# Deformable 3x3 convolution on one core: sampling in five matmuls instead of six, two row groups completed by small DMAs, and a new order of the steady iteration

## The chip, the cores and the metric

The kernel runs on one core of a Trainium2 chip. The metric is the device time of one execution in microseconds. Matrix products run on TensorE (PE, with its weight loads PEld), elementwise work on VectorE (DVE), ScalarE (ACT) and GpSimd (POOL), and DMAs are issued from the queues of SyncE (SP) and ScalarE (ACTq).

## The reference

Two layers on x of 64 images, 1024 channels, 14x14 pixels, all float32. Layer 0 is a residual bottleneck (1x1, 3x3, 1x1 convolutions with batch norms); it is done before the part that changes. Layer 1, cut to what matters:

```python
out = relu(group_norm(conv(x, w1)))                      # 1024 -> 256 channels
om = conv(out, w_off, pad=1) + b_off                     # 27 channels: 9 x offsets, 9 y offsets, 9 masks
py, px = grid_y + ky + off_y, grid_x + kx + off_x        # for each of K = 9 taps and 196 pixels
sampled = bilinear_sample(out, py, px) * sigmoid(mask)   # [256, 9, 14, 14] per image
out = einsum('bckhw,ock->bohw', sampled, w2)             # 9 taps x 256 channels -> 256
out = conv(relu(group_norm(out)), w3)                    # 256 -> 1024
return relu(group_norm(out) + x)
```

## The kernel before

Layer 1 is `deformable_phase`. It works on pairs of images (32 pairs), software-pipelined: `by_iteration` runs one `step` per pair, and each engine's `step` is a hand-written list of calls for the pairs `past`, `before`, `now`, `after`, `coming`. The order inside each engine is exactly that list; engines meet only through semaphores. (The pairs are named alike on every engine but shifted: what PE calls `now` and `after` in its last lines is `before` and `now` for ACT and DVE.)

Every product is made in three passes of float32r parts: a value is split by ACT into a high part and by DVE into the rest, and high x high, low x high and high x low are added in PSUM.

Bilinear sampling is a matrix product. For a pair, an image i and a group g of two taps (the fifth group has one), the matrix s of 196 source pixels x (2 taps x 196 target pixels) is the product of a "hat" in y and a "hat" in x. A unit u is one (g, i): nine units a pair, and the last holds the single tap of both images. A unit goes through these steps:

- `load_hats` (SP): the hats are read from DRAM (`hat_scratch`) and spread over the partitions, into one of three buffers `hats`. With the 196 pixels in two halves of 98 partitions (7 image rows of 14) that is three DMAs: y hats of each half, x hats.
- `make_s` (POOL for units 0, 1, 2, 6, 7, DVE for 3, 4, 5, 8) multiplies y hats by x hats.
- `part_s` (ACT) makes s_hi, `rest_s` (DVE) s_lo; the next load into the same buffer waits for s_lo.
- `sample_tile` t (PE), 20 a pair: t = 4g + 2i + c, c being the half of the 256 channels. The weights are aT, the image's activations transposed (`transposes`, `part_aT`, `rest_aT`), the moving operand is s. Six matmuls: two halves of the pixels by three products, each over 98 partitions. Tiles 0 to 15 have 392 columns, 16 to 19 have 196.
- `part_v` (ACT) and `rest_v` (DVE) take each tile out of PSUM; `deform_part` (PE) multiplies by w2.

A pair's hats begin when `spread_offsets` has spread the offsets: ACT makes distances, hats and mask, POOL multiplies the mask in (`mask_hats`), SP stores them to `hat_scratch` (`store_hats`), waits for that, and loads units 0, 1, 2. Around this, PE also does conv1 (`conv1` 0 to 7) of a later pair, the offset convolution (`offsets`), and the last 1x1 convolution (`conv3` 0 to 7) of an earlier one, with one small matmul for each group norm (`group_a`, `group_b`, `group_y`).

## Time and profile before

| | |
|---|---|
| median of 3 runs | 2962.01 us (2961.58 to 2963.43) |
| the profiled execution | 2961.04 us, span 2958.8 us |
| mean granted clock of TensorE | 0.994 |
| busy share PE, PEld, DVE, ACT, POOL | 98%, 97%, 80%, 61%, 15% |
| mean share of the 16 DMA engines | q1 (SP) 32.7%, q10 (ACTq) 11.8% |

The span runs from the first to the last instruction; the execution's own time is 2.2 us longer. The deformable stage fills the last two thirds, from about 960 us on, and is a steady iteration repeated for each pair.

### The profile page before, as it was taken

The numbers are of one execution on the slowest core, as the hardware profiler recorded it, in microseconds if no ns is written. First come the engines' busy times: TensorE is split into PE (matmuls) and PEld (weight loads), VectorE is DVE, ScalarE is ACT, GpSimd is POOL, SyncE is SP. The second block draws the span as 40 slices with busy tenths as digits, with TensorE's granted clock in tenths as the row PEclk, the third lists the DMA queues.
The fourth block names the chain that finished last, engine by engine and source line by source line (L and its number), as shares of the span: only waits on it lengthen the run. The fifth ranks groups of instructions, "written<-read, shape, count | busy, mean of one in ns | idle before, by whom it ended". The sixth has DMA issues, their size and how long they took to land.

```text
span 2958.8 us, 46593 instructions
## 1 busy us (share of the span) xinstructions
PE 2908.3 (98%) x16518; PEld 2865.9 (97%) x16518; DVE 2366.0 (80%) x5000; ACT 1795.0 (61%) x3281; POOL 455.3 (15%) x305
## 2 busy tenths in 40 slices
PE   9999999999998999999999999999999999999997
PEld 9999999999997899999999999999999999999997
DVE  5655889865666688888888888888888888888885
ACT  4544332346665466767666676676766767667664
POOL 0000000000000122221222212222122221222210
PEclk9999999999999899999999999999999999999998
DMA  7774111035663344444444444444544444444431
GB/s 270 215 238 134 44 44 40 10 124 218 245 232 130 122 136 152 156 150 158 150 153 154 148 159 151 153 155 150 158 150 156 152 149 159 148 152 156 149 121 74
DMA packets 209208, 437.39 MB, mean 148 GB/s; under 512 B 18640, under 2 KB 170192, under 8 KB 203344
## 3 DMA queue, kind: packets, MB, share of 16 engines
q1 hardware_dynamic: 159408, 326.82, 32.7%
q10 hardware_dynamic: 49568, 107.60, 11.8%
q8 instruction: 131, 2.15, 0.3%
q14 instruction: 101, 0.83, 0.1%
HBM read 307.71 MB, written 126.64 MB: 147 GB/s over the span
## 4 chain that ended last, share of the span: by engine, by line
PE 63%; DVE 3%; DMA 1%; ACT 1%; SPq 0%; issue 0%; POOL 0%; ACTq 0%; DVEq 0%; POOLq 0%
PE sample L87 7%; PE deform L87 7%; PE sample L88 7%; PE sample L92 7%; PE deform L92 7%; PE deform L88 6%; PE work L87 6%; PE work L92 6%; PE work L88 6%; PE work L74 1%; PE work L76 1%; PE work L75 1%; DMA hats<-hat_scratch 1%; PE work L2046 1%; DVE x L1715 1%; DVE s_lo L1819 1%
## 5 line engine op out<-in xcount | busy, mean ns | idle before, releaser
L1465 ACT ACTIVATE v_hi<-sample 128x392 fp32r<-128x392 f32 (+1 forms) x640 | 291.7, 463 | 315.1 <-PE sample L92 306.0
L87 PE MATMUL sample<-s_hi,aT_hi 98*128 98x392 f32 (+1 forms) x1280 | 417.5, 331 | 8.9 <-DVE v_lo L1827 8.9
L1675 POOL TENSOR_TENSOR hats<-hats 98x784 f32<-98x784 f32 x160 | 341.0, 2131 | 523.1 <-DMA hats<-hat_scratch 504.3
L88 PE MATMUL sample<-s_hi,aT_lo 98*128 98x392 f32 (+1 forms) x1280 | 413.3, 328 | 0.0
L87 PE MATMUL deform<-v_hi,w_w 128*128 128x392 f32 x1152 | 403.5, 350 | 0.0
L88 PE MATMUL deform<-v_hi,w_w 128*128 128x392 f32 x1152 | 393.1, 341 | 0.0
L1827 DVE TENSOR_TENSOR v_lo<-sample,v_hi 128x392 fp32r<-128x392 f32 (+1 forms) x640 | 326.9, 518 | 66.5 <-ACT v_hi L1465 62.2
L92 PE MATMUL sample<-s_lo,aT_hi 98*128 98x392 f32 (+1 forms) x1280 | 315.1, 327 | 0.0
L92 PE MATMUL deform<-v_lo,w_w 128*128 128x392 f32 x1152 | 310.4, 342 | 0.0
L1456 ACT ACTIVATE s_hi<-hats 98x784 fp32r<-98x784 f32 x288 | 245.4, 852 | 98.5 <-DVE x L1715 71.7
L1819 DVE TENSOR_TENSOR s_lo<-hats,s_hi 98x784 fp32r<-98x784 f32 x288 | 281.1, 976 | 2.4 <-ACT s_hi L1456 1.4
L87 PEld LDWEIGHTS sample<-s_hi,aT_hi 98*128 98x128 f32 x1280 | 241.6, 189 | 13.6 <-DVE v_lo L1827 6.1
L88 PEld LDWEIGHTS sample<-s_hi,aT_lo 98*128 98x128 f32 x1280 | 243.0, 190 | 0.1
L92 PEld LDWEIGHTS sample<-s_lo,aT_hi 98*128 98x128 f32 x1280 | 227.3, 189 | 0.3 <-DVE s_lo L1819 0.3
L88 PEld LDWEIGHTS deform<-v_hi,w_w 128*128 128x128 f32 x1152 | 217.8, 189 | 0.0
L87 PEld LDWEIGHTS deform<-v_hi,w_w 128*128 128x128 f32 x1152 | 217.6, 189 | 0.0
L1715 DVE SCALAR_TENSOR_TENSOR x<-in_home,scale,x 128x392 f32<-128x392 f32 x248 | 210.2, 848 | 5.5 <-DMA in_home<-y_scratch 5.5
L92 PEld LDWEIGHTS deform<-v_lo,w_w 128*128 128x128 f32 x1152 | 211.8, 188 | 0.0
L1843 DVE SCALAR_TENSOR_TENSOR x<-y_home,gn,x 128x196 f32<-128x196 f32 x496 | 208.5, 483 | 0.1
L1141 POOL TENSOR_TENSOR gn<-gn,half_neg 128x2 f32<-128x2 f32 x96 | 76.4, 796 | 810.0 <-DVE gn L1153 810.0
L1521 ACT ACTIVATE x<-x,gn 128x196 f32<-128x196 f32 x496 | 191.6, 447 | 1.0 <-issue 0.6
L1388 ACT ACTIVATE x<-x,shift 128x392 f32<-128x392 f32 x256 | 157.8, 616 | 46.4 <-DVE x L1715 33.2
(227 smaller groups left out, 7282.9 us busy)
## 6 DMA issues: line engine op xcount, KB each, us to landing
hats<-hat_scratch SPq DMA_DIRECT2D x768, 150.1 KB
x<-in_x SPq DMA_DIRECT2D x64, 784.0 KB, 5.8
in_home<-y_scratch ACTq DMA_DIRECT2D x248, 196.0 KB, 3.3
out<-x ACTq DMA_DIRECT2D x62, 784.0 KB, 4.4
y_home<-in_x SPq DMA_DIRECT2D x32, 784.0 KB, 5.0
y_scratch<-y_out SPq DMA_DIRECT2D x16, 1568.0 KB, 5.9
terms<-in_x SPq DMA_DIRECT2D x30, 784.0 KB, 4.7
y_scratch<-y_home SPq DMA_DIRECT2D x15, 1568.0 KB, 5.1
```

The lines of the kernel that those rows point to most:

```text
L87: nc.tensor.matmul(out, w_hi, x_hi, start=start, stop=False)
L88: nc.tensor.matmul(out, w_lo, x_hi, start=False, stop=False)
L92: return nc.tensor.matmul(out, w_hi, x_lo, start=False, stop=stop)
L1388: nc.scalar.activation(x1[:, p.buf, :, k, :], x1[:, p.buf, :, k, :], ACT.Relu, bias=shift[:, k:k + 1]).then_inc(x1_made, 1)
L1456: nc.scalar.activation(s_hi[:, unit % 2], hats[:, unit % HATS, 0:2], ACT.Copy).then_inc(s_hi_made, 1)
L1465: nc.scalar.activation(v_hi[:, group % 2, c, 0:taps_of(g), i, :], sample[:, t % 2, 0:cols(g)].rearrange("p (k s) -> p k s", s=PIX), ACT.Co ...
L1521: last = nc.scalar.activation(x1[:, p.buf, i, k, :], x1[:, p.buf, i, k, :], ACT.Relu, bias=gn3.shift[:, i, k:k + 1])
L1675: nc.gpsimd.tensor_tensor(hats[:, slot, 0:2, 0:n], hats[:, slot, 0:2, 0:n], hats[:, slot, 2:3, 0:n].broadcast_to([HALF, 2, n]), ALU.mult). ...
L1715: nc.vector.scalar_tensor_tensor(x1[:, p.buf, :, k, :], from_y, scale[:, k:k + 1], x1[:, p.buf, :, k, :], ALU.mult, ALU.add).then_inc(plus ...
L1819: nc.vector.tensor_tensor(s_lo[:, unit % 2], hats[:, unit % HATS, 0:2], s_hi[:, unit % 2].bitcast(F32), ALU.subtract).then_inc(s_lo_made, 1)
L1827: nc.vector.tensor_tensor(v_lo[:, group % 2, c, 0:taps_of(g), i, :], sample[:, t % 2, 0:cols(g)].rearrange("p (k s) -> p k s", s=PIX), v_h ...
L1843: last = nc.vector.scalar_tensor_tensor(x1[:, p.buf, i, k, :], y[:, i, k, :], gn3.scale[:, i, k:k + 1], x1[:, p.buf, i, k, :], ALU.mult, A ...
```

## The change

The 196 source pixels are no longer cut 98 + 98 but 126 + 70: 9 image rows and 5. The first group (A) keeps its three products. Of the second (R, 70 rows) the three products are packed into two matmuls. Plane 2 of the weights has the high part of aT on rows 0 to 69, and on rows 70 to 125 the low part of rows 0 to 55; its moving operand has s_hi of R on rows 0 to 69 and again s_hi of R's rows 0 to 55 on 70 to 125 (the y hats of those rows are loaded a second time, so `make_s`, `part_s` and `rest_s` make the copy with the same instructions, on 126 partitions instead of 98). Plane 3 has the high part on rows 0 to 69 with s_lo, and on rows 70 to 83 the low part of rows 56 to 69 with s_hi. What must cross partitions for this is moved by DMA from SBUF to SBUF: `copy_s`, 14 rows of 392 per unit, and `copy_aT`, 56 and 14 rows per image. The moved rows of s have semaphores of their own, taken over from the earlier phases (`first_loaded0` and `3`), those of aT use `last_counted`. Each hats load is four DMAs (9, 5 and 4 rows of y hats, x hats over 9 rows). `rest_aT` becomes two instructions, and the low part of R goes to `a_f`'s place first. The order of the steady iteration is another one on PE, ACT, DVE and SP (POOL's is the same); the first and the last iterations follow it.

```diff
-        aT_hi = sb("aT_hi", [HALF, 2, 2, CMID], F32R)
-        aT_lo = sb("aT_lo", [HALF, 2, 2, CMID], F32R)
+        aT = sb("aT", [A_ROWS, 2, 4, CMID], F32R)
...
-        hats = sb("hats", [HALF, HATS, 3, 2 * PIX])
-        s_hi = sb("s_hi", [HALF, 2, 2, 2 * PIX], F32R)
-        s_lo = sb("s_lo", [HALF, 2, 2, 2 * PIX], F32R)
+        hats = sb("hats", [A_ROWS, HATS, 3, 2 * PIX])
+        s_hi = sb("s_hi", [A_ROWS, 2, 2, 2 * PIX], F32R)
+        s_lo = sb("s_lo", [A_ROWS, 2, 2, 2 * PIX], F32R)
...
+                for i, at in parts:
+                    n = at.stop - at.start
+                    y_hat, x_hat = (hats_at[p.n % 2, e, i, :, t0:t0 + n] for e in range(2))
+                    for dst, rows in ((hats[:, slot, 0, at], slice(0, UPPER)), (hats[0:R_ROWS, slot, 1, at], slice(UPPER, SIDE)),
+                                      (hats[R_ROWS:A_ROWS, slot, 1, at], slice(UPPER, SIDE - 1))):
+                        sp.dma_start(dst, y_hat[rows].unsqueeze(1).broadcast_to([rows.stop - rows.start, SIDE, n])
                                      ).then_inc(hats_loaded[slot], 16)
...
+                    sp.dma_start(hats[:, slot, 2, at], x_hat.unsqueeze(0).broadcast_to([UPPER, SIDE, n])
                                  ).then_inc(hats_loaded[slot], 16)
...
+            @of_pair
+            def copy_s(p, u):
+
+                unit = UNITS * p.n + u
+                sp.wait_ge(s_lo_made, unit + 1)
+                sp.dma_start(s_lo[R_ROWS:C_ROWS, unit % 2, 1].bitcast(F32), s_hi[TWICE:R_ROWS, unit % 2, 1].bitcast(F32)
+                             ).then_inc(s_moved[unit % 2], 16)
+
+            @of_pair
+            def copy_aT(p, i):
+
+                sp.wait_ge(aT_lo_made, 2 * p.n + i + 1)
+                if i == 1:
+                    sp.wait_ge(aT_moved, aT_moved_before + 64 * p.n + 32)
+                for plane, rows in ((2, slice(0, TWICE)), (3, slice(TWICE, R_ROWS))):
+                    n = rows.stop - rows.start
+                    sp.dma_start(aT[R_ROWS:R_ROWS + n, i, plane].rearrange("p (k c) -> p k c", k=KM).bitcast(F32),
+                                 aT_rest[rows, :, i].bitcast(F32)
+                                 ).then_inc(aT_moved, 16)
...
-                for h in range(2):
-                    products_of_high(nc, sample[:, t % 2, 0:n], aT_hi[:, i, h, c * P:(c + 1) * P],
-                                     aT_lo[:, i, h, c * P:(c + 1) * P], s_hi[:, unit % 2, h, at:at + n], start=(h == 0))
+                to, a_part = sample[:, t % 2, 0:n], aT[:, i, :, c * P:(c + 1) * P]
+                high, low = s_hi[:, unit % 2, :, at:at + n], s_lo[:, unit % 2, :, at:at + n]
+                nc.tensor.matmul(to, a_part[:, 0], high[:, 0], start=True, stop=False)
+                nc.tensor.matmul(to, a_part[:, 1], high[:, 0], start=False, stop=False)
+                if t in (0, 2):
+                    pe.wait_ge(aT_moved, aT_moved_before + 64 * p.n + 32 * (i + 1))
+                nc.tensor.matmul(to, a_part[:, 2], high[:, 1], start=False, stop=False)
                 if c == 0:
                     pe.wait_ge(s_lo_made, unit + 1)
-                for h in range(2):
-                    last = product_of_low(nc, sample[:, t % 2, 0:n], aT_hi[:, i, h, c * P:(c + 1) * P],
-                                          s_lo[:, unit % 2, h, at:at + n], stop=(h == 1))
+                nc.tensor.matmul(to, a_part[:, 0], low[:, 0], start=False, stop=False)
+                if c == 0:
+                    pe.wait_ge(s_moved[unit % 2], s_moved_before[unit % 2] + 16 * (unit // 2 + 1))
+                last = nc.tensor.matmul(to, a_part[0:C_ROWS, 3], low[0:C_ROWS, 1], start=False, stop=True)
```

SP's list of the steady iteration, where every `copy_` line is new and `load_x` moved:

```diff
             def step(past, before, now, after, coming):
+                copy_s(now, 1)
                 load_hats(now, 4)
+                copy_s(now, 2)
                 load_hats(now, 5)
+                copy_s(now, 3)
+                load_x(coming, 0)
+                copy_s(now, 4)
                 load_hats(now, 6)
                 load_hats(now, 7)
-                load_x(coming, 0)
+                copy_s(now, 5)
+                load_x(coming, 1)
                 load_hats(now, 8)
-                load_x(coming, 1)
                 store_hats(after, 1, 0)
+                copy_s(now, 6)
                 store_hats(after, 1, 1)
+                copy_s(now, 7)
                 store_hats(after, 0, 0)
                 store_hats(after, 0, 1)
                 load_hats(after, 0)
+                copy_s(now, 8)
                 load_hats(after, 1)
                 load_hats(after, 2)
+                copy_aT(after, 0)
+                copy_s(after, 0)
                 load_hats(after, 3)
+                copy_aT(after, 1)
```

One 392-column sample tile on PE, the first of a unit, before (in brackets what it waits for):

```order
L87 MATMUL sample<-s_hi,aT_hi 128x392 [waits v_lo_made,s_hi_made]
L88 MATMUL sample<-s_hi,aT_lo 128x392
L87 MATMUL sample<-s_hi,aT_hi 128x392
L88 MATMUL sample<-s_hi,aT_lo 128x392
L92 MATMUL sample<-s_lo,aT_hi 128x392 [waits s_lo_made]
L92 MATMUL sample<-s_lo,aT_hi 128x392
```

The same on PE after the change, tile 0 of a pair, where the wait for the moved rows of aT (`last_counted`) and of s (`first_loaded0`) stands too:

```order
L2107 MATMUL sample<-s_hi,aT 128x392 [waits v_lo_made,s_hi_made,aT_lo_made]
L2108 MATMUL sample<-s_hi,aT 128x392
L2111 MATMUL sample<-s_hi,aT 128x392 [waits last_counted]
L2114 MATMUL sample<-s_lo,aT 128x392 [waits s_lo_made]
L2117 MATMUL sample<-s_lo,aT 128x392 [waits first_loaded0]
```

One matmul is gone, and the tile has two waits that end only with a DMA.

SP's queue from the last hats store of a pair to the load of unit 3, before:

```order
L1339 DMA hat_scratch<-offs_b 9x14x196 [waits masked] x2
L1327 DMA hats<-hat_scratch 98x1x392 [waits hats_stored0,s_lo_made]
L1327 DMA hats<-hat_scratch 98x1x392
L1330 DMA hats<-hat_scratch 98x1x392
L1327 DMA hats<-hat_scratch 98x1x392 [waits hats_stored1,s_lo_made]
L1327 DMA hats<-hat_scratch 98x1x392
L1330 DMA hats<-hat_scratch 98x1x392
L1327 DMA hats<-hat_scratch 98x1x392 [waits s_lo_made]
L1327 DMA hats<-hat_scratch 98x1x392
L1330 DMA hats<-hat_scratch 98x1x392
```

The same place on SP after the change, from the load of unit 1 to the first copy of s, with the copy of unit 8 of the pair before ahead of it:

```order
L1345 DMA s_lo<-s_hi 14x392 [waits s_lo_made]
L1335 DMA hats<-hat_scratch 126x1x392 [waits hats_stored1,s_lo_made]
L1335 DMA hats<-hat_scratch 70x1x392
L1335 DMA hats<-hat_scratch 56x1x392
L1337 DMA hats<-hat_scratch 126x1x392
L1335 DMA hats<-hat_scratch 126x1x392 [waits s_lo_made]
L1335 DMA hats<-hat_scratch 70x1x392
L1335 DMA hats<-hat_scratch 56x1x392
L1337 DMA hats<-hat_scratch 126x1x392
L1356 DMA aT<-in_home 56x2x128 [waits aT_lo_made]
L1356 DMA aT<-in_home 14x2x128
L1345 DMA s_lo<-s_hi 14x392 [waits s_lo_made]
```

Four DMAs stand where three stood, and the three small moves for sample tile 0 stand behind the twelve of units 0, 1 and 2.

## Rows read from the trace of the kernel before

**Rows 1.** Page, part 1: busy time of the engines over the whole span.
```profile
span 2958.8 us, 46593 instructions
PE 2908.3 (98%) x16518; PEld 2865.9 (97%) x16518; DVE 2366.0 (80%) x5000; ACT 1795.0 (61%) x3281; POOL 455.3 (15%) x305
```

**Rows 2.** Windows: length, busy us PE, PEld, DVE, ACT, POOL, PEclk, DMA share, GB/s.
```profile
2000.00:2250.00 250.00, 250.00 (x1466) 248.79 (x1465) 217.90 (x512) 174.25 (x356) 58.26 (x38) 1.00 0.48 153
```

**Rows 3.** Waits, 2000 to 2250 us: us in total, times, longest.
```profile
POOL hats L1675 <- DMA hats<-hat_scratch: 68.0, 18, 7.7
DVE v_lo L1827 <- ACT v_hi L1465: 5.3, 10, 1.4
```

**Rows 4.** Timeline of PE: start, us, engine, line, operation.
```profile
2000.06 0.34 PE L88 MATMUL deform<-v_hi,w_w 128*128 128x392 f32 x1
2000.24 0.34 PE L87 MATMUL deform<-v_hi,w_w 128*128 128x392 f32 x1
...
2000.96 0.25 PE L87 MATMUL sample<-s_hi,aT_hi 98*128 98x196 f32 x1
...
2001.61 0.27 PE L87 MATMUL sample<-s_hi,aT_hi 98*128 98x196 f32 x1
...
2007.93 0.34 PE L87 MATMUL sample<-s_hi,aT_hi 98*128 98x392 f32 x1
...
2009.01 0.34 PE L87 MATMUL sample<-s_hi,aT_hi 98*128 98x392 f32 x1
...
2049.42 0.34 PE L2035 MATMUL work<-x_hi,select_s 96*126 96x392 f32 x1
...
2062.53 0.26 PE L87 MATMUL sample<-s_hi,aT_hi 98*128 98x196 f32 x1
```

**Rows 5.** Groups by line and form, whole span.
```profile
L87 PE MATMUL sample<-s_hi,aT_hi 98*128 98x392 f32 x1024 | 355.6, 347 | 8.9 <-DVE v_lo L1827 8.9
```

**Rows 6.** Timeline of SPq: issues of stores, hats loads and an x load.
```profile
2037.32 0.45 SPq L1302 DMA_DIRECT2D x<-in_x  x1
...
2050.48 3.16 SPq L1339 DMA_DIRECT2D hat_scratch<-offs_b  x4
2054.77 1.55 SPq L1327 DMA_DIRECT2D hats<-hat_scratch  x2
2056.36 0.73 SPq L1330 DMA_DIRECT2D hats<-hat_scratch  x1
```

**Rows 7.** Timeline of POOL: `make_s` of units 0, 1, 2.
```profile
2060.75 1.88 POOL L1675 TENSOR_TENSOR hats<-hats 98x784 f32<-98x784 f32 x1 [7.37 <-DMA hats<-hat_scratch]
2064.52 1.89 POOL L1675 TENSOR_TENSOR hats<-hats 98x784 f32<-98x784 f32 x1 [1.89 <-DMA hats<-hat_scratch]
2067.36 2.59 POOL L1675 TENSOR_TENSOR hats<-hats 98x784 f32<-98x784 f32 x1 [0.94 <-DMA hats<-hat_scratch]
```

**Rows 8.** Timeline of DVE: L1715 alone and beside POOL, the split of aT.
```profile
2020.73 0.62 DVE L1715 SCALAR_TENSOR_TENSOR x<-in_home,scale,x 128x392 f32<-128x392 f32 x1
...
2061.16 1.90 DVE L1715 SCALAR_TENSOR_TENSOR x<-in_home,scale,x 128x392 f32<-128x392 f32 x1
...
2064.74 0.69 DVE L1801 TENSOR_TENSOR aT_lo<-work,aT_hi 98x512 fp32r<-98x512 f32 x1 [0.63 <-ACT aT_hi L1448]
2065.35 0.35 DVE L1827 TENSOR_TENSOR v_lo<-sample,v_hi 128x196 fp32r<-128x196 f32 x1
```

**Rows 9.** Windows of 2 us, columns as in rows 2.
```profile
2055.00:2057.00 2.00, 2.00 (x13) 2.00 (x12) 2.00 (x6) 1.97 (x5) 0.00 (x0) 1.00 0.45 135
2057.00:2059.00 2.00, 2.00 (x14) 1.95 (x14) 2.00 (x6) 1.97 (x6) 0.00 (x0) 1.00 0.45 140
...
2089.00:2091.00 2.00, 2.00 (x13) 2.00 (x13) 0.98 (x1) 0.99 (x2) 0.00 (x0) 1.00 0.94 329
```

**Rows 10.** DMA view, 2000 to 2250 us: packets, queues, issues (KB each, median us to landing).
```profile
DMA packets 22078, 38.28 MB, mean 153 GB/s; under 512 B 1778, under 2 KB 20008, under 8 KB 22056
...
in_home<-y_scratch ACTq DMA_DIRECT2D x33, 196.0 KB, 3.2
```

More of the change, by code:

```diff
@@ L1563, in second @@
                 part_a(after)
+                part_v(now, 6)
                 part_s(now, 5)
@@ L1864, in second @@
                 rest_s(now, 1)
-                make_s(now, 3)
+                rest_s(now, 2)
                 rest_v(now, 0)
@@ L1905, in step @@
                     return second(now, after, coming)
+                rest_x1(after, 1)
+                add_y(after, 3)
+                add_y(after, 4)
+                rest_s(now, 0)
                 rest_v(before, 16)
+                rest_v(before, 17)
                 rest_aT(now, 0)
-                rest_v(before, 17)
-                add_y(after, 3)
-                rest_x1(after, 1)
-                rest_s(now, 0)
+                add_x1(past, 5)
+                add_x1(past, 6)
                 rest_v(before, 18)
+                rest_aT(now, 1)
@@ L1913, in step @@
                 rest_v(before, 19)
-                add_x1(past, 5)
+                add_y(after, 5)
+                rest_s(now, 1)
+                add_x1(past, 7)
                 rest_x1(after, 2)
-                add_y(after, 4)
-                rest_aT(now, 1)
-                rest_s(now, 1)
+                rest_x1(after, 3)
+                add_y(after, 6)
+                rest_s(now, 2)
                 rest_v(now, 0)
                 rest_v(now, 1)
-                rest_x1(after, 3)
-                make_s(now, 3)
@@ L2133, in step @@
                     fresh = None
+                first = coming is not None and coming.n == 0
                 sample_tile(now, 16)
@@ L2155, in step @@
                 sample_tile(after, 5)
-                deform_part(after, 0, 1)
-                group_b(now)
-                if now is not None and now.n == PAIRS - 1:
-                    keep_warm(nc, sample[:, 0, 0:PAIR], w1.hi_flat, 26)
-                deform_part(after, 0, 2)
-                conv1(fresh, 4)
                 conv1(fresh, 5)
-                deform_part(after, 0, 3)
                 conv1(fresh, 6)
                 conv1(fresh, 7)
-                sample_tile(after, 6)
+                deform_part(after, 0, 1)
                 conv3(now, 0)
                 conv3(now, 1)
-                first = coming is not None and coming.n == 0
                 if first:
@@ L2175, in step @@
                 conv3(now, 2)
+                if now is not None and now.n == PAIRS - 1:
+                    keep_warm(nc, sample[:, 0, 0:PAIR], w1.hi_flat, 26)
+                deform_part(after, 0, 2)
                 conv3(now, 3)
+                conv3(now, 4)
+                sample_tile(after, 6)
                 sample_tile(after, 7)
-                conv3(now, 4)
-                sample_tile(after, 8)
-                deform_part(after, 1, 0)
                 conv3(now, 5)
```

279 lines of the change are left out of this document (141 added, 138 removed).

## The prediction

> **What bounds the kernel now.** I read the page's busy times first: PE has 98% of the span, DVE 80%, ACT 61% [rows 1]. An average over stages proves little, so next the windows of the deformable stage: over 250 us PE is busy for all 250 at full clock, DVE for 217.9 (87%), ACT for 174, and the DMA engines have a mean share of 0.48 [rows 2]. A busy PE can still hide waits, so the list of waits in that window: no row has PE as the one who waits; POOL waits for its hats, DVE 5.3 us for ACT [rows 3]. The timeline says the same: 392-column matmuls start 0.18 us apart, and tile 16 of one pair starts at 2000.96, that of the next at 2062.53 [rows 4]. So an iteration is **61.57 us**, all of it PE's matmul stream.
>
> **What goes.** A 392-column tile took 6 matmuls in 2009.01 - 2007.93 = 1.08 us, 0.18 each; a 196-column one 2001.61 - 2000.96 = 0.65 us, 0.108 each [rows 4]. One matmul of each goes. A pair has 16 wide tiles and 4 narrow ones: 1024 records of the wide form are 512 wide tiles with two halves each [rows 5], and 32 pairs have 128 narrow ones. 16 x 0.18 + 4 x 0.108 = 3.31 us per pair, **106 us** in all. A PE-bound iteration is then 61.57 - 3.31 = 58.26 us. That the five run over 126 rows of weights (the last over 84) instead of 98 I cost at nothing: deform's matmuls over 128 rows start 0.18 us apart too [rows 4]. If every one cost 5% more, 100 matmuls x 0.009 = 0.9 us a pair would come back.
>
> **What is added on DVE.** The same instructions on 126 partitions instead of 98 have the same columns; nothing. `rest_aT` becomes two instructions of 256 columns: 512 columns took 0.69, 196 took 0.35 [rows 8], so a line through both gives 0.41 each, 0.13 more per image, 0.26 per pair. DVE goes from 217.9 / 250 x 61.57 = 53.7 to 53.9 us of 58.26, or 93%. Its idle time falls from 7.9 to 4.3 us. Part of the busy time is collision: `add_y` (L1715) takes 0.62 alone and 1.90 when it starts 0.4 us after a POOL multiply, ending 0.4 us after that one's end [rows 7, 8]. The new order moves these calls about; one collision more or less is some 1.3 us, and with 4.3 us of idle time I take it as hidden.
>
> **What is added on SP.** A hats load issued three DMAs in 1.55 + 0.73 = 2.28 us; four stores took 3.16, an x load 0.45 [rows 6]. Now 8 units x 4 + 8 = 40 hats DMAs x 0.76 = 30.4, 3.2 for stores, 0.9 for x. The 9 copies of s and 4 of aT have no row: from 0.45 (plain x load) to 0.79 (one store), 6 to 10 us; I take 0.45 for s, plain like the x load, and 0.7 for aT, three-dimensional like hats: 6.9. Sum 41 us of 58: not a bound, but each unit is issued 0.76 us later.
>
> **What is added on the DMA engines.** With only hats moving, the share is 0.45 at 135 to 140 GB/s, against 0.94 at 329 GB/s when full rows move [rows 9]. 0.45 x 16 = 7.2: a hats DMA (7 image rows of 14 partitions) works on seven engines, and a backlog of further hats DMAs does not widen it to others. The small packets confirm it: 1778 under 512 B in 250 us are 438 per iteration [rows 10], and 30 hats DMAs x 7 + 4 stores (9 groups) x 9 + 12 others x 16 is exactly 438. At 137 GB/s one hats DMA (98 rows of 1568 B, 154 KB) takes 1.12 us. By the same pattern the new ones split in groups of 9, 5, 4 and 9 engines with 14 rows each, again 1.12 us. If the four meet on the same engines, a unit takes 4.5 us instead of 3.4. If they spread, about 3.4 remains; I take the first, since the seven never changed in the backlog.
>
> The Trainium skill has this as a rule (DMA: Bandwidth & Descriptors, section "Why a DMA increments its semaphore by 16 and not by 1"): a DMA from SP or ACT is split over the largest number up to 16 that divides the slowest dimension of both sides, and on the lowest-numbered engines. By it engines 0 to 3 carry all four DMAs, so it speaks against this change; the trace agrees on the number (7.2 of 16 by share), and cannot show which ones.
>
> Load of the fullest engine, per iteration: hats before 24 x 1.12 + 6 x 0.56 = 30.2 us. An x load or an output store of an image (803 KB) at 329 GB/s is 2.44 us on all 16, four of them 9.8; eight y loads of 201 KB, 4.9; stores 2.2. Sum 47.1 of 61.57 (76%). After: hats 32 x 1.12 + 8 x 0.56 = 40.3, copies about 1, sum **58.2 of 58.26**. Taken literally this is a second bound at the same height. It is an upper estimate: peaks of a busy stretch count gaps between DMAs as work, and 0.94 was not full. Spread evenly the new bytes would be far below. I do not let it set the time, but it is the place where the forecast can break.
>
> **The tight chain: from the offsets to tile 0.** Before: the last spread matmul at 2049.42; the first hats load is issued at 2054.77, 5.35 later; unit 2 is landed when POOL starts on it at 2067.36, 12.6 us after that [rows 4, 6, 7]. Tile 0 of the pair started 2007.93 - 2000.96 = 6.97 into its iteration, so at 2062.53 + 6.97 = 2069.50: 20.1 us after the spread. After: counting the matmuls of PE's new list at 0.18, the last spread is at 42.8 and tile 0 at 8.1 of the next iteration, 58.26 - 42.8 + 8.1 = 23.6 us. SP's first load now stands behind two copies of s (units 6 and 7), and hats are made after the mask: I count 1.9 us more, 7.2. Three units take 12.6 + 3 x 1.12 = 16.0. The copies of aT and of s for tile 0 are issued behind them and land no earlier, some 0.5 us later: 7.2 + 16.0 + 0.5 = 23.7. PE asks for them at its third and fifth matmul, 23.6 + 0.36 and + 0.72. That leaves 0.3 us for aT: no cover. The smallest landing in the trace is 3.2 us for 196 KB [rows 10], and 14 rows can hardly be slower; SP issues them when DVE has finished `rest_aT`, about 4 us ahead of need, so alone they fit. What is late next, if they are late, is tile 0, and with it everything behind on PE, 1 for 1. Similar short covers: the group_b matmul, which now stands 5.0 us (before 8.6) behind the last `deform_part` whose result must be copied, counted and reduced; and tile 18, which needs rest of tile 16 while `rest_s(0)` stands in front. I take **0.5 us of PE stall per iteration** for all, 31 x 0.5 = 15 us; bounds 0 and 3.3 (gain gone).
>
> **Sum.** 2961.0 of the profiled execution - 106 + 15 = 2870; that run is 1 us under the median, so **2871 us** on it, 3.1% faster.
>
> **The rivals.**
> A. The chain is later than I counted: DMAs of the hats or the small moves come 1 to 2.5 us late each iteration. For it: 58.2 of 58.26 on the fullest engine, and covers under 1 us. Against: POOL, DVE and ACT have room to take up jitter. At 1.5 us a pair, 2856 + 31 x 1.5 = 2903; span 2887 to 2935.
> B. DVE becomes the bound. If its forced idle time stays at 7.9 us although the order is new, the iteration is 53.9 + 7.9 = 61.8 and nothing is won; if it shrinks to 6, 59.9 us, 2856 + 51 = 2907. It decides above 4.3 us. Against: most of its idle time stood in waits for a PE that will be faster.
> C. Slower: the fullest DMA engines set the period. 36 wide-equivalents of hats DMA plus 17.9 us of the rest pass 61.57 at 1.21 us each, 8% above 1.12. At 1.25 the iteration is 62.9, 2962 + 32 x 1.3 = 3004. Against: 1.12 already has gaps in it, and it needs all four DMAs of a unit on the same engines. The Trainium skill's rule named above would put them there.
> D. The gain isn't there: five matmuls with 126 rows cost what six did. 2962. Against: deform's cadence with 128 rows.
>
> **How the numbers follow.** Forecast (stall 0 to 1 us a pair, 2856 to 2887) 0.65; A 0.20; B 0.08, of which 0.02 ends within 0.2%; C 0.05; D 0.02, half within 0.2%, half slower. Faster by over 0.2% (6 us, about what a measurement of this kernel tells from no change) 0.65 + 0.20 + 0.06 = 0.91; within it 0.02 + 0.01 = 0.03; slower 0.05 + 0.01 = 0.06. The range is 2852 to 2925: below, no stall and the 9 us that PE waited for v_lo over the whole span [rows 5] half gone; above, most of A and B.
>
> **What would show it.** Matmul records of tiles with five members 0.18 us apart; `transposes` or tile 16 repeating every 58.3 to 59.3 us; DVE about 92% busy in steady windows; DMA share about 0.6 and hats-only stretches above 0.45; POOL starting units 0, 1, 2 about 4.5 us apart. A stall shows as an idle row before the sample matmuls with a DMA as its releaser (chain, A), before group sums or sample with DVE (B). The forecast is wrong if the iteration is over 59.5 us, and most likely so if the copies of tile 0 land after the hats of unit 2 by more than 1 us.

## The result, and the profile after

The changed kernel takes **2986.39 us** (median of 4 runs, 2980.93 to 2989.8) against 2961.8 for the kernel before on the same chip: a ratio of 1.0081 (95% interval 1.0063 to 1.0098), so 0.8% slower. The profiled execution took 2985.33 us, of which 2983.1 are the span. The forecast was 2871, faster.

The page after, part 1, and the 250 us window of the deformable stage (columns as in [rows 2]):

```profile
span 2983.1 us, 46209 instructions
PE 2847.9 (95%) x15878; PEld 2753.8 (92%) x15878; DVE 2397.7 (80%) x5064; ACT 1807.6 (61%) x3345; POOL 463.3 (16%) x305
```

```profile
2000.00:2250.00 250.00, 240.43 (x1368) 232.09 (x1367) 220.90 (x521) 174.03 (x361) 56.35 (x36) 1.00 0.57 176
```

PE lost 60 us of work over the span, and the span grew by 24: what was all work in [rows 2] now has nearly 10 us of gaps in 250. (A matmul that starts after a wait is shown longer, 0.45 instead of 0.34 us in a row below, so busy PE fell by less than the work that went.) Who waits for what over the steady stage, 1250 to 2750 us: in total us, times, longest. First the engines, then SP's queue:

```profile
POOL hats L1716 <- DMA hats<-hat_scratch: 689.6, 121, 13.3
...
PE sample L2107 <- DVE v_lo L1871: 28.2, 42, 1.4
...
PE sample L2117 <- DMA s_lo<-s_hi: 20.4, 33, 1.8
...
PE sample L2111 <- DMA aT<-in_home: 10.3, 19, 1.0
```

```profile
SPq L1345 <- DVE s_lo L1863: 226.0, 87, 9.3
SPq L1356 <- DVE in_home L1845: 63.0, 24, 3.4
```

59 us of PE's gaps in 1500 have three releasers, none dominant: the rest of an earlier tile (`v_lo`; a tile may only be written once the tile two before it has been taken out), the moved rows of s, those of aT. For PE the same list of the kernel before holds 1.1 us for `v_lo` and nothing else. SP now waits at L1345 (`copy_s`, for `s_lo`) and L1356 (`copy_aT`, for the rest of R), with stores and loads of the next pair queued behind it. One iteration in detail. SP after, the columns of [rows 6]:

```profile
2058.54 0.80 SPq L1366 DMA_DIRECT2D hat_scratch<-offs_b  x1
2059.38 0.81 SPq L1345 DMA_DIRECT2D s_lo<-s_hi  x1
2060.23 0.76 SPq L1366 DMA_DIRECT2D hat_scratch<-offs_b  x1
2061.04 1.04 SPq L1345 DMA_DIRECT2D s_lo<-s_hi  x1
2062.12 1.57 SPq L1366 DMA_DIRECT2D hat_scratch<-offs_b  x2
2064.83 2.21 SPq L1335 DMA_DIRECT2D hats<-hat_scratch  x3
...
2067.88 0.83 SPq L1345 DMA_DIRECT2D s_lo<-s_hi  x1
...
2074.10 0.75 SPq L1337 DMA_DIRECT2D hats<-hat_scratch  x1
2077.91 1.76 SPq L1356 DMA_DIRECT2D aT<-in_home  x2
2079.72 0.81 SPq L1345 DMA_DIRECT2D s_lo<-s_hi  x1
```

POOL, DVE and PE in the same iteration (their timelines, one fence each):

```profile
2058.59 1.02 POOL L1723 TENSOR_TENSOR offs_b<-offs_b 126x392 f32<-126x392 f32 x1 [1.97 <-ACT offs_b L1475]
...
2072.54 2.20 POOL L1716 TENSOR_TENSOR hats<-hats 126x784 f32<-126x784 f32 x1 [11.27 <-DMA hats<-hat_scratch]
```

```profile
2072.39 2.78 DVE L1756 SCALAR_TENSOR_TENSOR x<-in_home,scale,x 128x392 f32<-128x392 f32 x2
2075.67 0.97 DVE L1863 TENSOR_TENSOR s_lo<-hats,s_hi 126x784 fp32r<-126x784 f32 x1 [0.50 <-ACT s_hi L1497]
...
2077.47 0.41 DVE L1845 TENSOR_TENSOR in_home<-work,aT 70x256 fp32r<-70x256 f32 x1
```

```profile
2077.06 0.33 PE L2107 MATMUL sample<-s_hi,aT 126*128 126x196 f32 x1 [0.83 <-DVE v_lo L1871]
...
2082.17 0.34 PE L2108 MATMUL sample<-s_hi,aT 126*128 126x392 f32 x1
2082.42 0.45 PE L2111 MATMUL sample<-s_hi,aT 126*128 126x392 f32 x1
```

Read as one chain: the mask product at 2058.59; four stores with two copies of s between them, done at 2063.69; first load at 2064.83; unit 0's product at 2072.54, and beside it two `add_y` that take 2.78 us instead of some 1.2; `s_lo` of unit 0 only at 2075.67, in front of the rest of tile 16 and the rest of R. So PE waits 0.83 us at 2077.06, where tile 18 needs the rest of tile 16, and SP stands from 2074.85 to 2077.91 until it may copy aT. Tile 0's third matmul is the first to read that copy; it starts at 2082.42, 0.25 us after the one at 2082.17 instead of 0.18, so here the copy came 0.07 us late. Tile 18 of the pair before waited likewise and started at 2014.18, so this iteration takes 62.9 us where 58.8 were forecast. This chain ends in only a part of its waits: between the two starts PE also waits 0.67 us for aT, 0.29 for `v_lo`, and 1.08 and 0.34 for copies of s.

### The profile page after: what moved, and what is told of

It reads as the page before. It is cut to its first block, busy times and chain, and to the rows that moved or that the text cites. A ratio compares the mean times of both kernels' runs of the same rounds, so it can differ in the third digit from the quotient of the medians.

```text
span 2983.1 us, 46209 instructions
## 1 busy us (share of the span) xinstructions
PE 2847.9 (95%) x15878; PEld 2753.8 (92%) x15878; DVE 2397.7 (80%) x5064; ACT 1807.6 (61%) x3345; POOL 463.3 (16%) x305
## 4 chain that ended last, share of the span: by engine, by line
PE 32%; DMA 14%; SPq 8%; DVE 8%; ACT 4%; issue 2%; POOL 2%; ACTq 0%; POOLq 0%; DVEq 0%
DMA s_lo<-s_hi 6%; PE work L92 4%; PE work L97 4%; PE work L93 4%; SPq L1335 3%; DMA hats<-hat_scratch 3%; PE deform L92 3%; PE deform L97 3%; PE deform L93 3%; DVE s_lo L1863 3%; PE sample L2117 2%; DMA aT<-in_home 2%; SPq L1356 2%; PE sample L2111 2%; PE sample L2107 2%
## 5 line engine op out<-in xcount | busy, mean ns | idle before, releaser
L1716 POOL TENSOR_TENSOR hats<-hats 126x784 f32<-126x784 f32 x160 | 328.8, 2055 | 922.1 <-DMA hats<-hat_scratch 922.1
L1863 DVE TENSOR_TENSOR s_lo<-hats,s_hi 126x784 fp32r<-126x784 f32 x288 | 311.8, 1083 | 34.4 <-ACT s_hi L1497 34.4
L1497 ACT ACTIVATE s_hi<-hats 126x784 fp32r<-126x784 f32 x288 | 245.9, 854 | 84.8 <-POOL hats L1716 79.8
L2107 PE MATMUL sample<-s_hi,aT 126*128 126x392 f32 (+1 forms) x640 | 216.3, 338 | 42.1 <-DVE v_lo L1871 41.9
L2117 PE MATMUL sample<-s_lo,aT 84*128 84x392 f32 (+1 forms) x640 | 218.4, 341 | 33.8 <-DMA s_lo<-s_hi 33.3
L2111 PE MATMUL sample<-s_hi,aT 126*128 126x392 f32 (+1 forms) x640 | 215.1, 336 | 14.4 <-DMA aT<-in_home 14.1
L97 PEld LDWEIGHTS deform<-v_lo,w_w 128*128 128x128 f32 x1152 | 211.8, 188 | 0.0
L2108 PE MATMUL sample<-s_hi,aT 126*128 126x392 f32 (+1 forms) x640 | 210.2, 328 | 0.0
L2114 PE MATMUL sample<-s_lo,aT 126*128 126x392 f32 (+1 forms) x640 | 210.2, 328 | 0.0
L1756 DVE SCALAR_TENSOR_TENSOR x<-in_home,scale,x 128x392 f32<-128x392 f32 x248 | 188.0, 768 | 13.9 <-DMA in_home<-y_scratch 13.5
L1146 POOL TENSOR_TENSOR gn<-gn,half_neg 128x2 f32<-128x2 f32 x96 | 97.0, 1010 | 601.5 <-DVE gn L1158 601.5
L92 PE MATMUL work<-b_hi,w3b_w 128*128 128x392 f32 x512 | 179.3, 350 | 4.9 <-ACT b_hi L1531 4.9
L2107 PEld LDWEIGHTS sample<-s_hi,aT 126*128 126x128 f32 x640 | 121.6, 190 | 62.7 <-issue 56.4
```

Source lines behind the costliest of these rows:

```text
L92: nc.tensor.matmul(out, w_hi, x_hi, start=start, stop=False)
L97: return nc.tensor.matmul(out, w_hi, x_lo, start=False, stop=stop)
L1497: nc.scalar.activation(s_hi[:, unit % 2], hats[:, unit % HATS, 0:2], ACT.Copy).then_inc(s_hi_made, 1)
L1716: nc.gpsimd.tensor_tensor(hats[:, slot, 0:2, 0:n], hats[:, slot, 0:2, 0:n], hats[:, slot, 2:3, 0:n].broadcast_to([A_ROWS, 2, n]), ALU.mult ...
L1863: nc.vector.tensor_tensor(s_lo[:, unit % 2], hats[:, unit % HATS, 0:2], s_hi[:, unit % 2].bitcast(F32), ALU.subtract).then_inc(s_lo_made, 1)
L2107: nc.tensor.matmul(to, a_part[:, 0], high[:, 0], start=True, stop=False)
```

## The experiments

Each kernel was timed against the kernel before on the same chip (2960 to 2961 us). "Period" is a median over 21 to 23 iterations, 1300 to 2700 us, from one mask product on POOL to the next; it is 61.56 us in the kernel before and 61.97 after (means 61.7 and 62.1). From the first to the last mask product the change costs 13 us of its 24; the other 11 lie behind the last one, where the pipeline runs out.

**1. Which part costs: the moves, the lists, or the five matmuls.** The edits are applied to the changed kernel.

```diff
 no_copy_s:  def copy_s(p, u):   + return      ; PE's wait on s_moved left out
 no_copy_aT: def copy_aT(p, i):  + return      ; PE's and ACT's waits on aT_moved left out
-    a_part[:, 2], high[:, 1]   ...  a_part[0:C_ROWS, 3], low[0:C_ROWS, 1]
+    a_part[0:R_ROWS, 2], high[0:R_ROWS, 1] ... a_part[0:R_ROWS, 3], low[0:R_ROWS, 1]
 no_copies:  both
```

> The changed kernel without both kinds of small move (the 9 copies of s and the 4 of aT per pair) and without PE's waits for them; the third and fifth matmul of a tile run over 70 rows, so part of the low products is left out. Theory 1 (the moves land late because they stand in SP's queue behind hats loads, and PE waits for them): most of the loss goes, 2860 to 2895 us. Theory 2 (the four hats DMAs of a unit share their engines, so the hats themselves are late): the hats still hold tile 0, 2930 to 2970. Theory 3 (the new order on DVE and ACT is the bound, the moves are innocent): 2970 to 2990.

> Only the copies of s and PE's wait for them are left out (the fifth matmul multiplies whatever low part stands on the 14 rows); those of aT stay. Theory 1: the copies of s are nine of the moves and the ones the last chain names most, so more than half of the difference goes, 2890 to 2930 us. Theory 2: 2950 to 2975. Theory 3: 2970 to 2990.

> Only the copies of aT and the waits for them are left out; the low products of the second group are left out with them, the third and fifth matmul run over 70 rows, and the nine copies of s stay as DMAs with PE's wait. Theory 1: tile 0 and tile 2 wait less, SP is free 3.5 us earlier before unit 3, 2940 to 2965 us. Theory 2: 2960 to 2980. Theory 3: 2970 to 2990.

Measured: without any move **2897.44** us (0.9793, 0.9776 to 0.9809), without those of s 2902.59 (0.9808, 0.9794 to 0.9823), without those of aT 2965.44 (1.0019, 1.0008 to 1.003). The moves cost 89 us; those of s alone 84, those of aT alone 21, so together less than the sum. The first is 2 us above theory 1's range, the last is just past theory 1's and inside theory 2's. (Without the moved rows a part of the low products of R is left out too; the number of matmuls stays five.) SP's issues without moves:

```profile
2068.24 3.13 SPq L1368 DMA_DIRECT2D hat_scratch<-offs_b  x4
2072.70 2.19 SPq L1335 DMA_DIRECT2D hats<-hat_scratch  x3
```

The mask product stood at 2068.30 there: 4.4 us to the first load, against 6.2 above. Over all iterations the medians are 4.50 without moves, 4.55 with those of aT alone, 5.99 after. The period is 59.25, 59.50 and 61.97.

The rest, 2897 against 2871, made the lists themselves suspect. So the new lists alone, with the six matmuls, buffers and three loads of before; and the reverse, packing and moves in the lists of before, each copy put in ahead of a load.

> The kernel before with the new order of the lists on PE, ACT, DVE and SP and nothing else: six matmuls, 98 + 98 partitions, three hats DMAs, no copies. Theory 1 (the order is innocent): PE has 3.3 us more work per pair and covers what it covered, 2960 to 2968 us. Theory 2 (the order itself brings waits of 1 us or more per pair): 2985 to 3010.

> The changed kernel (five matmuls, 126 partitions, four hats DMAs, all copies) with the lists of the kernel before, the copies put into SP's list each where its wait is met first. If the new order was needed to hide the moves (theory 1 with the order as a help): slower than the change, 3000 to 3050 us. If the new order was made for other latencies than the chip has and hurts (theory 2): faster than the change, 2930 to 2975.

Measured: the lists alone **3002.68** us (1.0142, 1.0127 to 1.0157), 41 us slower than before, as theory 2 had it. The packing in the old lists 3502.33 (1.1828, 1.1809 to 1.1848): slower than either theory, since PE waits for over half of the moves of s, up to 6.2 us each. The old lists have no room for them.

```profile
PE sample L2117 <- DMA s_lo<-s_hi: 251.5, 111, 6.2
```

Step by step that is 2961 + 41 (lists) - 105 (3003 to 2897: five matmuls, 126 partitions, the fourth load) + 89 (moves) = 2986. These are differences along one row of kernels, so they must add up; it is no proof that each term would have this size elsewhere, and part 2 shows that it doesn't.

**2. What in the lists costs.** POOL of the run with the lists alone, then DVE:

```profile
2021.92 1.95 POOL L1675 TENSOR_TENSOR hats<-hats 98x784 f32<-98x784 f32 x1 [1.03 <-DMA hats<-hat_scratch]
...
2060.31 1.88 POOL L1675 TENSOR_TENSOR hats<-hats 98x784 f32<-98x784 f32 x1 [1.51 <-DMA hats<-hat_scratch]
```

```profile
2022.06 2.78 DVE L1715 SCALAR_TENSOR_TENSOR x<-in_home,scale,x 128x392 f32<-128x392 f32 x2
2024.76 0.96 DVE L1819 TENSOR_TENSOR s_lo<-hats,s_hi 98x784 fp32r<-98x784 f32 x1
2025.65 0.62 DVE L1827 TENSOR_TENSOR v_lo<-sample,v_hi 128x196 fp32r<-128x196 f32 x2
...
2060.43 2.59 DVE L1819 TENSOR_TENSOR s_lo<-hats,s_hi 98x784 fp32r<-98x784 f32 x1
```

```profile
2026.14 0.33 PE L87 MATMUL sample<-s_hi,aT_hi 98*128 98x196 f32 x1 [0.62 <-DVE v_lo L1827]
```

In these rows a VectorE operation with both operands in SBUF that starts inside a product of GpSimd ends only after it: `s_lo` from 60.43 to 63.02, where the product ended at 62.19 and `s_lo` alone takes 0.97. The Trainium skill has the lock (SBUF — State Buffer, section "SBUF: two separate sides"): whichever of the two starts first keeps the shared port pair for its whole instruction, against a VectorE operation with two SBUF inputs. The trace agrees, and also on the exception: after, the rest of aT (one operand in PSUM, L1842) started at 2077.14, 0.05 us into the product of 2077.09, and took its normal 0.41. First I moved the two `add_y` that stand ahead of `rest_s(now, 0)` behind it:

```diff
-                add_y(after, 3)
-                add_y(after, 4)
                 rest_s(now, 0)
                 rest_v(before, 16)
+                add_y(after, 3)
                 rest_v(before, 17)
                 rest_aT(now, 0)
+                add_y(after, 4)
```

> The six-matmul kernel in the new order (3003 us) with one change of DVE's list: add_y(3) behind rest_v(16) and add_y(4) behind rest_aT(0), instead of both ahead of rest_s(0) and rest_v(16). If the 41 us of the new order come from this place (a POOL multiply holds up the two add_y, and tile 18 waits for the rest of tile 16 behind them): 2962 to 2975 us. If they come from elsewhere: 2990 to 3005.

> The changed kernel with the same change of DVE's list, nothing left out. If both costs add (89 us of moves, 41 of the order): 2940 to 2955 us. If the late moves only take the place of what the list no longer costs, 2975 to 2990.

> The same change of DVE's list in the kernel without small moves (2897 us; low products partly left out). If the place named is all that was left of the new order's cost: 2858 to 2870 us, the stall-free sum. If the hats' fourth DMA holds PE too: 2875 to 2890. If the place is innocent: 2895 to 2900.

All three expectations missed: 3044.69 (1.0284, 1.0265 to 1.0304) with the lists alone, 3044.35 (1.0283, 1.0254 to 1.0313) with the change, 2913.51 (0.984, 0.9825 to 0.9855) without moves, 42, 58 and 16 us worse than the same kernels unedited. The lists alone show what was new: in 1250 to 2750 us ACT waits 64.9 us for the late `add_y` ahead of `v_hi`, a row that the unedited kernel doesn't have:

```profile
ACT v_hi L1465 <- DVE x L1715: 64.9, 22, 3.8
```

Place was the wrong lever, so the next edit makes the product itself short:

```diff
-                nc.gpsimd.tensor_tensor(hats[:, slot, 0:2, 0:n], hats[:, slot, 0:2, 0:n],
-                                        hats[:, slot, 2:3, 0:n].broadcast_to([HALF, 2, n]), ALU.mult)
+                nc.gpsimd.tensor_tensor(hats[:, slot, 0:2, 0:49], hats[:, slot, 0:2, 0:49],
+                                        hats[:, slot, 2:3, 0:49].broadcast_to([HALF, 2, 49]), ALU.mult)
```

> The six matmuls of the kernel before in the new lists, without moves (3003 us), with GpSimd's product of the hats over 49 of the 392 columns alone; the other columns keep the row's own hat, so the samples are wrong sums. If the new order's 41 us come from VectorE operations that are held while GpSimd multiplies, they go: 2955 to 2970 us. If they come from the place of operations on VectorE or ScalarE alone, they stay: 2990 to 3003.

> The kernel before with the same short product (49 of 392 columns), the control to the run with the new lists. Both theories: 2950 to 2962 us, since TensorE has nearly no idle time there. What the new order costs without the long product is the difference of the two: near 0 if the held VectorE operations are the cause, near 41 us if not.

> The changed kernel, moves and all, with GpSimd's product of the hats over 49 of the 392 columns alone; the other columns keep the row's own hat, so the samples are wrong sums. SyncE's queue, the DMAs and all waits are those of the change. If the moves cost only together with the long product (it makes s_lo late, SyncE waits for s_lo, and the hats behind it come late), then nothing but the short waits of TensorE for a move is left over 2849: 2850 to 2885 us. If the moves cost 89 us on their own, only the new order's 49 us go: 2925 to 2950.

> The same short product (49 of 392 columns) with the moves of s and aT left out too, and the rows of the fourth and fifth matmul that they would fill: five matmuls in the new lists and nothing else; the samples are wrong sums. If five matmuls save the 3.31 us per pair of tiles of the arithmetic, 106 us, from the 2954 of the six with the short product: 2845 to 2855 us, with TensorE hardly waiting. If VectorE becomes the bound of a 58 us iteration by itself: 2875 or more.

| us | product as it is | short product |
|---|---|---|
| lists of before, six matmuls | 2960 to 2962 | 2954.69 (0.9981, 0.9972 to 0.9991) |
| new lists, six matmuls | 3002.68 | 2953.57 (0.9978, 0.9969 to 0.9987) |
| new lists, five, no moves | 2897.44 | 2865.33 (0.9678, 0.9662 to 0.9694) |
| new lists, five, moves | 2986.39 | 2943.82 (0.9948, 0.9931 to 0.9965) |

The first theory holds: with the short product the lists cost nothing (2953.6 against 2954.7), and the window of the second row has no gap left:

```profile
2000.00:2250.00 250.00, 250.00 (x1462) 248.87 (x1461) 207.67 (x515) 175.93 (x359) 32.53 (x36) 1.00 0.49 153
```

A short product also ends sooner, so that s could be made sooner. The traces speak for the hold. In 1250 to 2750 us of the lists alone DVE waits 34.9 us for `s_hi` with the long product and 30.2 with the short one, while `s_lo` falls from 1096 to 977 ns in the mean and `add_y` from 787 to 635.

Not all of the 41 us is waiting. In the same 1500 us of the lists alone PE waits 24.8 us for `v_lo`, the longest 2.4, and TensorE's granted clock is at 1.2 instead of 2.4 GHz in four stretches, which is worth up to another 10.3 us (the shortfall of PEclk, summed over windows of 2 us); one stretch begins behind a wait of 2.29 us that ends at 2153.10. The kernel before, the changed kernel and the four kernels with the short product have no such stretch there.

The third row comes near what the forecast described: 2865, a period of 58.54 us, though 10 us above the 2845 to 2855 expected of it. The moves cost 78 us there too: their cost does not hang on the product. But it takes another form there. PE's waits of the fourth row (changed kernel, short product), 1250 to 2750 us:

```profile
PE sample L2111 <- DMA aT<-in_home: 23.7, 26, 1.9
PE sample L2117 <- DMA s_lo<-s_hi: 11.1, 23, 1.6
```

No wait for `v_lo` is left. The mean period is 60.59 us here and 58.60 in the third row's run, which makes 49 us in that stretch. 35 of them are PE itself waiting for moved rows, and two thirds of the 35 for those of aT, at tile 0 of nearly every pair.

**3. How the moves cost.** First the copies of s issued from ACT's queue, then the copies issued as they are but not waited for by PE (ACT and DVE wait for the copy of two units before, and the fifth matmul reads 70 rows alone):

```diff
 copy_s_from_act
-                sp.dma_start(s_lo[R_ROWS:C_ROWS, unit % 2, 1].bitcast(F32), ...
+                act.dma_start(s_lo[R_ROWS:C_ROWS, unit % 2, 1].bitcast(F32), ...
 copy_s_aside
-                if c == 0:
-                    pe.wait_ge(s_moved[unit % 2], s_moved_before[unit % 2] + 16 * (unit // 2 + 1))
```

> The changed kernel with the nine copies of s per pair issued from ScalarE's queue, each some ACT operations behind the s_hi of its unit, so that they stand in other rings than the hats loads; the copies of aT stay on SP. Theory 1 in its narrow form (a copy is late because it stands behind hats DMAs in the same queue): a copy lands in 2 to 3 us, 2905 to 2940 us. Theory 1 in its wide form (it shares the busy DMA engines, whichever queue it comes from): 2955 to 2985. If ACT's own waits for s_lo cost more than the queue did: over 2990.

> All DMAs of the changed kernel, the nine copies of s too, but PE doesn't wait for them (its fifth matmul reads only 70 rows, so a part of the low products is left out; ACT and DVE wait for the copy of two units before, long landed). It parts the wait for a copy from its load. If PE's wait is the cost (latency): as without the copies of s, 2900 to 2912 us. If it is the room they take in SP's queue and on the DMA engines, which delays the hats: 2965 to 2990.

From ACT's queue: 2994.89 (1.0114, 1.0098 to 1.0129), 8 us slower than the change, although SP was relieved: its first load comes 4.2 us behind the mask product, as without the copies of s. PE waits 40.7 us in 1500 for s there, against 20.4. It is the third branch of the expectation, but that it is ACT's own waits for `s_lo` that cost is not separated from the copies' later issue. Two of its copies in the chain of waits:

```profile
2001.02 2.71 DMA s_lo<-s_hi
2017.98 5.53 DMA s_lo<-s_hi
```

A copy is 21 KB. The first was issued where the engines had little to do (share 0.30 from 2001 to 2003), the second behind the loads of two units (share 0.68 from 2018 to 2023): 2.7 us against 5.5. In the changed kernel, from SP's queue, the copies in the chain take 3.9 to 5.8. So its latency goes by how busy the DMA engines are with what was issued before, from either queue. The Trainium skill states that DMAs started by the scalar, sync or gpsimd engine all run on the same 16 DMA engines and interleave (DMA: Bandwidth & Descriptors, section "Issuing engines are not separate DMA queues"); the 5.5 us behind loads of the other queue agree. Aside: 2978.29 (1.0055, 1.004 to 1.007). Leaving out PE's wait for s thus gives back 8 of the 84 us; the first load comes 6.91 us behind the mask product in that run, and PE's other waits grew (39.1 us for `v_lo` in 1500, 18.1 for group sums). So neither way out helps by itself: without the entries in SP's queue the change stays at 2995, without PE's wait at 2978, without both it is 2903. By what share each costs stays open. Two more tried to part place from load on the DMA engines:

```diff
 stores_first
-  store(1,0) copy_s(6) store(1,1) copy_s(7) store(0,0) store(0,1) load 0 copy_s(8) load 1 load 2
+  store(1,0) store(1,1) copy_s(6) store(0,0) store(0,1) copy_s(7) load 0 load 1 copy_s(8) load 2
 loads_on_14
-  source rows 9, 5, 4, 9, each repeated 14 (9) times
+  source rows 42, 14, 14, 42, each repeated 3, 5, 4, 3 times
```

> The changed kernel, with the three small moves of s that stand among the stores and first loads of the next pair's hats put behind them by one place (store, store, move, store, store, move, load, load, move, load). Nothing is left out. If the moves cost by their place in SyncE's queue, where each holds up the stores and loads behind it while it waits for s_lo, this gives back a good part of the 76 us that a move costs without TensorE waiting for it: 2930 to 2965 us. If they cost by the work on the DMA engines, place alone gives little: 2975 to 2990. If TensorE then waits for the moves put back, 2990 or more.

> The changed kernel, in which each load of the hats reads its bytes as 42, 14, 14 and 42 rows, each repeated 3, 5, 4 and 3 times, in place of 9, 5 and 4 rows repeated 14 times and 14 rows repeated 9 times. The bytes written are as many, but they are not those of the hats, so the samples are wrong sums; the instructions, waits and queues are the same. If each DMA spreads over as many DMA engines as divide its rows, all four then run on 14 engines and the loads land much earlier than 5.3 us after issue. If the loss comes by the fullest DMA engines: 2900 to 2940 us. If it comes by the places in SyncE's queue: 2975 to 2990.

stores_first: **3063.8** (1.0351, 1.0334 to 1.0369), far into the third branch of its expectation. The first load did come earlier (5.38 us behind the mask product, median), but copy 8, now behind two loads, landed 6.8 us after its issue, and PE stood 4.15 us for it:

```profile
2043.90 0.83 SPq L1345 DMA_DIRECT2D s_lo<-s_hi  x1
```

```profile
2050.78 0.53 PE L2117 MATMUL sample<-s_lo,aT 84*128 84x196 f32 x1 [4.15 <-DMA s_lo<-s_hi]
```

So a move costs wherever it stands: ahead of the loads it delays them, behind them it lands late. PE waits 94.0 us for s in 1500 there, and on top of that comes the clock. Windows of that wait and behind it (columns as in [rows 2]):

```profile
2048.00:2050.00 2.00, 0.00 (x0) 0.00 (x0) 1.90 (x3) 0.86 (x1) 0.01 (x1) 0.80 0.50 159
2052.00:2054.00 2.00, 2.00 (x8) 2.00 (x8) 0.49 (x3) 1.52 (x5) 0.00 (x0) 0.50 0.31 77
2056.00:2058.00 2.00, 2.00 (x17) 2.00 (x16) 0.36 (x1) 0.89 (x2) 1.69 (x1) 1.00 0.16 43
```

While PE stands, the granted clock falls to 1.2 GHz (PEclk 0.50), and it is back at 2.4 GHz at 2056; in between 392-column matmuls start 0.33 us apart instead of 0.18. Over 1250 to 2750 us the shortfall of PEclk is worth up to 39 us in this run, 38 in add_y_later, 19 in order_alone_add_y_later, 20 in loads_on_14 and 5 in copy_s_aside. These kernels are thus slower by more than their waits.

loads_on_14: 3013.82 (1.017, 1.0143 to 1.0197), outside both ranges. Its DMA view against that of the changed kernel, same 250 us:

```profile
DMA packets 27725, 43.91 MB, mean 176 GB/s; under 512 B 2738, under 2 KB 25656, under 8 KB 27704
```

```profile
DMA packets 28380, 42.67 MB, mean 171 GB/s; under 512 B 3810, under 2 KB 26439, under 8 KB 28359
```

Small packets per iteration are 2738 x 61.97 / 250 = 679 and 3810 x 63.83 / 250 = 973. Counting one for each engine that a DMA uses, as the prediction did, 9, 5, 4 and 9 for the hats give 680, 14 for each give 970, which is what whole iterations hold on average (680.4 and 970.0): the loads did spread. Unit 2's product came 14.7 us after the first load instead of 17.1, though the first load came 1.1 us later behind the mask product, so 1.3 us are left of the 2.4. Yet the kernel was 27 us slower, with 32 us of PE waits for s and 28 for group sums in 1500 us, and up to 20 us of clock. The earlier hats met other VectorE operations: `add_taps` (L1840) averages 1646 ns there against 556 in the changed kernel. So this run doesn't clear the fullest engines of the 89 us. That they don't bound the period is shown by the runs without moves, which load the same hats and have 59.25 and 58.54 us.

**4. Three loads instead of four**, the second plane taking y rows 5 to 13 in one DMA (other rows than the packing needs):

```diff
-   ((hats[:, slot, 0, at], slice(0, UPPER)), (hats[0:R_ROWS, slot, 1, at], slice(UPPER, SIDE)),
-    (hats[R_ROWS:A_ROWS, slot, 1, at], slice(UPPER, SIDE - 1)))
+   ((hats[:, slot, 0, at], slice(0, UPPER)), (hats[:, slot, 1, at], slice(LOWER, SIDE)))
```

> The changed kernel with three hats DMAs per unit instead of four: the second plane is loaded by one DMA of nine image rows (5 to 13) over all 126 partitions, so the second group is computed from wrong y hats; every instruction on PE, ACT, DVE and POOL and all small moves stay. It takes away 2 of the 8 DMAs that stand before a move, and a quarter of the hats' work on the fullest engines. Theory 1: moves land some 2 us earlier where a backlog stands, 2900 to 2940 us. Theory 2: the hats land as early as before the change, 2870 to 2910 us. Theory 3: 2970 to 2990.

> Both of the last two edits together: no small moves and no waits for them, and three hats DMAs per unit (wrong y hats for the second group, parts of the low products left out). Theory 1 (moves that land late plus a fourth hats DMA are all of the loss): the two gains add, the rest of 41 us over a stall-free 2856 goes, 2856 to 2870 us. Theory 2 (a third cause, the new order with its collisions between POOL's and DVE's work, holds PE too): it stays near the run without copies, 2885 to 2900.

With moves 2940.26 (0.9935, 0.992 to 0.995), 46 us better than the change; without them 2915.34 (0.9848, 0.9833 to 0.9863), 18 us worse than four loads without moves. Both fall outside their ranges, the first by 0.3 us, and the two gains don't add. Earlier hats help where hats are late: with moves PE waits only 1.7 us for s and 1.4 for aT in 1500. Elsewhere they put POOL's products beside other VectorE operations: in the first of them `add_taps` averages 1766 ns instead of 556, a step of the group sums (L1127) takes 1.01 us beside the mask product instead of 0.20, and PE waits 31.6 us for group sums. A kernel that computes the reference with three loads was not tried: the rows 9 to 12 would have to lie twice in `hat_scratch`.

## Why the prediction was wrong

- **"106 us" for the matmul: right in kind, too high by 0.2 to 0.4 us a pair.** The pair with the long product gives 105 us, but that difference also holds the waits and the 10.3 us of clock of the lists alone. The pair with the short product, where PE hardly waits, gives 88: the period falls from 61.41 to 58.54 us, 2.87 instead of 3.31. Start times of the tiles there give 3.1 (wide ones 1.07 and 0.90 us, narrow ones 0.66 and 0.55); the rest is not traced. Five matmuls of 126, 126, 70 or 84 rows keep 0.18 us each, so rival D is out.
- **"One collision more or less ... I take it as hidden": the first step that failed.** It was priced at nothing and cost 41 us. DVE's busy share did not decide (211.8 of 250 in the lists alone, 217.9 before; [rows 2]). The sum of the holds hardly did: `add_y` averages 787 ns there against 856 before, `s_lo` 1096 against 975, which by an estimate from 0.62 and 0.97 us for those not held is 59 us of hold in 1500 against 48, while the period's mean grew by 1.4 us, 34 in 1500. It fits that the place of a hold decides: now it is `s_lo`, or the `add_y` in front of it, and the rest of tile 16 queues behind, with less slack than one hold of 1.3 us. The short product shows that the holds are the cause; that their place is what makes them cost is argued from the rows of part 2.
- **The tight chain, "7.2 + 16.0 + 0.5 = 23.7" against 23.6 with "no cover": the second.** Its mechanism was seen and its terms were too small. In the medians of the changed kernel the last spread to the first load takes 7.95 us instead of 7.2 (6.48 without moves), because a copy of s takes 0.78 to 0.83 us of SP (1.04 in two cases) and not 0.45, and two stand ahead. The first load to unit 2's product takes 17.1 instead of 16.0. Together that is 25.1, 1.5 us past the 23.6 at which PE asks. SP was "not a bound" and stood in waits for 289 of 1500 us (its two rows above), which did not help, since the next pair's stores and loads stand behind the wait.
- **"Land no earlier, some 0.5 us later": right.** With the short product the copies of aT that PE waited for at tile 0 landed 0.3 to 0.6 us after the start of unit 2's product in 20 of 21 cases. In the changed kernel they came as close in the iteration shown (2082.4 against 2082.07). What made them late there is the chain ahead, and once more the late `s_lo`: SP stands until the rest of R is made. "0.5 us of PE stall per iteration" for all was 3.7: 61.97 less 58.26.
- **DMA, 1.12 us for each of four on the same engines: right in kind**, as the 17.1 us say. **Rival C** named the right sign but not the mechanism: the fullest engines did not set the period, which is 58.54 us with the same hats loads where moves and holds are out.
- **Rival A** (chain later by 1.5 us) was the right mechanism for the moves, and its 1.5 us is what this chain was late by; its 2903 has neither the holds nor the waits for s in it. **Rival B** fell: DVE was not full, but its order hurt.

The sign was reversed by two misses in one direction together; with one of them alone the kernel is still faster than before: 2897 us without the moves, 2944 with the moves and the short product.

Shown are the differences 41, 105 and 89 us, that the 41 come from POOL's long product, and that leaving out PE's own wait for s gives back 8 of the 84. How the 89 divide among the later first load, the landing of s and aT, the wait for the rest of R and loads 1 and 2 behind copy 8 stays open: each run that moved one of them moved others as well. Of the kernels with the whole computation none beat the one before.

## What to carry to other kernels

When TensorE is full, removing a matmul is worth its cadence only if every chain that feeds it keeps its slack. Count the slack of each chain at the new period; here a chain of 24 us with 0.3 us of cover had two terms that were 0.75 and 1.1 us too small. A DMA of 21 KB inside SBUF cost 0.8 us of an in-order queue and 2.1 to 8.7 us of latency in these runs, so price it at the busiest point of the queue. When an order is changed, look at what stands beside each GpSimd product with two SBUF operands, and what queues behind it, not at how many such pairs there are. And when a variant is slower than its waits explain, read the granted clock before giving the difference a cause.

## What was not expected of the hardware

- `s_lo` held for 1.6 us (2.59 instead of 0.97) by a GpSimd product of 1.88, while in the changed kernel an operation with one PSUM operand beside such a product ran undisturbed (0.41).
- A 21 KB copy inside SBUF took from 2.1 to 8.7 us (both with the packing in the old lists), more behind other DMAs than without, and ACT's queue was no way round.
- Spreading the same bytes over 14 DMA engines instead of 9, 5, 4 and 9 brought unit 2 2.4 us nearer to the first load, and the kernel was 27 us slower.
- In a wait of 4.15 us TensorE's clock fell to 1.2 GHz, and the matmuls behind it ran at that clock until 2056; such stretches were worth up to 39 of the 1500 us in stores_first, while the changed kernel had none in its 1500.
